# A fused Mamba and mixture-of-experts block on one core: the taps' row spread by full-height products, a lead for each spread of B, the last steps in halves, new slot tables

## What is computed

```
x  = L0_attn_x;  xn = layernorm(x)                 # 2048 tokens, 128 features
# Mamba block
xz = rmsnorm(xn) @ W_in; xi, z = split(xz)         # 256 channels each
xc = silu(conv4(xi) + conv_b)                      # causal taps along the tokens
dt, B, C = split(xc @ W_x);  dt = softplus(dt @ W_dt + b_dt)
h[t] = exp(dt * A) * h[t-1] + dt * xc * B          # 256 channels x 16 states
y  = (sum over states of h * C) + D_skip * xc
s  = xn + (y * silu(z)) @ W_out
# experts: top 2 of 8, all 8 computed, weighted by score
g  = silu(sum_e score_e * (relu(xn @ W1[e] + b1[e]) @ W2[e] + b2[e]))
out = x + s * g
```

## Time and profile before

| | us |
|---|---|
| median of 3 runs (lowest, highest) | 294.17 (293.43, 294.26) |
| the profiled execution's own time | 294.09 |
| its span, first to last instruction | 292.3 |
| busy in the span: PE, DVE, POOL, ACT | 268.1, 261.3, 241.0, 228.5 |

### The profile page before, as it was taken

The page is one execution under the profiler, slowest core; times in us unless marked ns, Lnnn a source line. Parts: engine busy times, 40 slices in busy tenths (PEclk is TensorE's granted clock), DMA queues, the critical chain, the costliest instruction groups (busy, mean ns, idle before and its releaser), DMA issues. The chain is left out here.

```text
span 292.3 us, 4275 instructions
## 1 busy us (share of the span) xinstructions
PE 268.1 (92%) x1237; PEld 137.2 (47%) x1237; DVE 261.3 (89%) x317; ACT 228.5 (78%) x444; POOL 241.0 (82%) x202
## 2 busy tenths in 40 slices
PE   7999989699999899699999999698999998999992
PEld 5543434255556345137474734124566443655461
DVE  4578999919999999979999797979999999999993
ACT  1377896989979885989998957989987875698630
POOL 5407986848999996757999999798999997799984
PEclk9999999989999999889999999899999999999998
DMA  6938672024029104724282005733049860000002
GB/s 181 278 79 192 149 177 58 2 59 102 9 54 208 31 0 108 182 71 86 51 183 64 0 2 126 162 99 61 7 100 207 189 153 0 2 0 2 2 1 72
DMA packets 18615, 25.65 MB, mean 88 GB/s; under 512 B 6440, under 2 KB 11935, under 8 KB 18592
## 3 DMA queue, kind: packets, MB, share of 16 engines
q1 hardware_dynamic: 17970, 24.71, 36.1%
q0 software_dynamic: 192, 0.52, 0.8%
q10 hardware_dynamic: 430, 0.14, 0.2%
HBM read 8.13 MB, written 1.31 MB: 32 GB/s over the span
## 5 line engine op out<-in xcount | busy, mean ns | idle before, releaser
L431 POOL TENSOR_TENSOR hc<-hs,Ct 128x1024 f32<-128x1024 f32 x63 | 149.1, 2379 | 12.6 <-DVE hs L979 12.3
L979 DVE TENSOR_TENSOR_SCAN hs<-dec,pdbu 128x1024 f32<-128x1024 f32 x64 | 144.1, 2274 | 0.9 <-POOL hc L431 0.5
L627 ACT ACTIVATE dec<-rep,negA 128x512 f32<-128x512 f32 x126 | 86.8, 723 | 3.0 <-DVE hs L979 2.3
L965 DVE TENSOR_TENSOR pdbu<-rep,px 128x1024 f32<-128x1024 f32 x62 | 73.5, 1218 | 12.4 <-PE px L1180 11.0
L1223 PEld LDWEIGHTS px<-w,hT 128*128 128x128 f32 x512 | 60.9, 192 | 17.5 <-issue 9.1
L1217 PE MATMUL px<-xnT,w 128*128 128x512 f32 x128 | 65.6, 614 | 1.6 <-DVE pdbu L965 0.9
L1223 PE MATMUL px<-w,hT 128*128 128x128 f32 x512 | 63.8, 278 | 1.3 <-ACT hT L760 0.9
L760 ACT ACTIVATE hT<-px,cols 128x512 f32<-128x512 f32 x64 | 43.9, 693 | 5.8 <-PE px L1217 5.5
L749 ACT ACTIVATE ysc<-px,score 128x128 f32<-128x128 f32 x116 | 33.1, 368 | 13.0 <-PE px L1223 12.8
L570 POOL TENSOR_TENSOR acc<-acc,ysc 128x512 f32<-128x512 f32 x29 | 37.6, 1298 | 6.5 <-ACT ysc L749 6.3
L1098 PE MATMUL py<-hc,rsel 128*32 128x512 f32 x256 | 35.6, 605 | 0.6 <-POOL hc L431 0.6
(11 more groups left out here) (171 smaller groups left out, 295.3 us busy)
## 6 DMA issues: line engine op xcount, KB each, us to landing
rep<-dt_u SPq DMA_DIRECT2D x116, 128.0 KB, 2.4
Ct<-bc_rows SPq DMA_DIRECT2D x16, 256.0 KB, 4.9
w<-in_L_ffn_W SPq DMA_DIRECT2D x1, 1024.0 KB
out<-xn SPq DMA_DIRECT2D x4, 256.0 KB, 2.5
x_sb<-in_L_attn_x SPq DMA_DIRECT2D x1, 768.0 KB, 5.6
rep<-dt_u POOLq DMA_DIRECT2D x4, 128.0 KB, 3.7
win<-in_L_attn_W_in SPq DMA_DIRECT2D x1, 256.0 KB, 3.0
bc_rows<-dtp SPq DMA_DIRECT2D x4, 64.0 KB, 1.6
```

What stands on the lines that cost most here:

```text
L431: eng.tensor_tensor(hc[:, n % HC_RING], hs[:, n % HS_RING], Ct[:, k % 2, j:j + 1, :].to_broadcast([P, 2, CH]), ALU.mult).then_inc(hc_last ...
L627: act.activation(dec[:, n % DEC_RING, i, :], rep[:, q, 0, :], ACT.Exp, scale=negA[:, q, j:j + 1])\
L965: dve.tensor_tensor(pdbu[:, at:at + 2, :], rep[:, 2 * pair:2 * pair + 2, 1, :], B[:, None, :].to_broadcast([P, 2, CH]), ALU.mult).then_inc ...
L979: dve.tensor_tensor_scan(hs[:, n % HS_RING].rearrange("p b t -> p (b t)"), dec[:, n % DEC_RING].rearrange("p b t -> p (b t)"), pdbu[:, at: ...
```

## The change

1. **Row of taps.** The buffer `hc[:, 0]`, whose first partition holds the row, is set to zero by a new first instruction of DVE; ACT's load of the row waits for it (`row_zero`), and with it the four loads behind it on ACT's queue. PE multiplies a square of ones with all 128 partitions, instead of one row with one row. The idle products are 3 instead of 6 ahead of it, and 2 new ones stand behind `tr`.
2. **DVE at the start.** The taps of channels 0 to 127 (`weigh_taps(0)`) and `rsel` go behind the first convolution.
3. **ACT at the start.** `Ln` goes ahead of the copy of B.
4. **AHEAD** becomes a list with a value for each spread, 0 to 4: nine spreads are issued one or two slots earlier (1, 12, 13, 15, 16, 18, 20, 21, 26), six one or two later (2, 8, 10, 19, 27, 31).
5. **The last chunk's end in halves of 256 tokens:** the last product with C, its reductions, the gate, `o` (one half in a bank of `pdbu`), POOL's and DVE's products and sums, and two output DMAs of half the size.
6. **Tables:** many jobs and steps move by a few slots.

```
-    "gate_y": [23, 40], "last_table": [40],
+    "gate_y": [23, 37], "last_table": [35],
...
-AHEAD = 2
+AHEAD = [2, 3, 1, 2, 2, 2, 2, 2, 1, 2, 1, 2, 3, 4, 2, 3, 3, 2, 3, 1, 4, 3, 2, 2, 2, 2, 3, 1, 2, 2, 2, 0]
...
-BUSY = {"row": 6, "xc1": 2}
+BUSY = {"row": 3, "tr": 2, "xc1": 2}
...
-    SLOTS.setdefault(4 * m - AHEAD, []).insert(0, ("B", m))
+    SLOTS.setdefault(4 * m - AHEAD[m], []).insert(0, ("B", m))
...
-            for k in range(CHUNKS):
-
-                sp.wait_ge(*((o_done, k + 1) if k < CHUNKS - 1 else (last_done, 1)))
+            for k in range(CHUNKS - 1):
+                sp.wait_ge(o_done, k + 1)
                 sp.dma_start(ov_dram[:, k * TPC:(k + 1) * TPC, :], xn[:, k]).then_inc(stored, 16)
-            sp.wait_ge(stored, 16 * CHUNKS)
+            k = CHUNKS - 1
+            for h in range(2):
+                i = slice(h * TPC // 2, (h + 1) * TPC // 2)
+                sp.wait_ge(last_done, h + 1)
+                sp.dma_start(ov_dram[:, k * TPC + i.start:k * TPC + i.stop, :], xn[:, k, i]).then_inc(stored, 16)
+            sp.wait_ge(stored, 16 * (CHUNKS + 1))
...
-            pool.tensor_tensor(s_sb[:, k, :], s_sb[:, k, :], acc[:, k % 2, :], ALU.mult).then_inc(last_sg_done, 1)
-            pool.wait_ge(last_sg_done, 1)
-            pool.tensor_tensor(s_sb[:, k, :], s_sb[:, k, :],
-                               x_sb[:, k].rearrange("p t d -> p (t d)"), ALU.add).then_inc(base_done, 1)
+            for h in range(2):
+                t = slice(h * CH // 2, (h + 1) * CH // 2)
+                pool.tensor_tensor(s_sb[:, k, t], s_sb[:, k, t], acc[:, k % 2, t], ALU.mult).then_inc(last_sg_done, 1)
+                pool.wait_ge(last_sg_done, h + 1)
+                pool.tensor_tensor(s_sb[:, k, t], s_sb[:, k, t],
+                                   x_sb[:, k].rearrange("p t d -> p (t d)")[:, t], ALU.add).then_inc(base_done, 1)
...
+            act.wait_ge(row_zero, 1)
             act.dma_start(cw_row.rearrange("p a b -> p (a b)"), conv_w.rearrange("d a k -> a (d k)")).then_inc(w_row, 16)
...
+            dve.memset(hc[:, 0, :, :], 0.0).then_inc(row_zero, 1)
...
             weigh_taps(1)
-            weigh_taps(0)
...
+            def times_C_last():
+
+                n = UNITS - 1
+                k, j, _ = place(n)
+                dve.wait_ge(scan_done, n + 1)
+                dve.wait_ge(reduced, (n - HC_RING) // 2 + 1)
+                for h in range(2):
+                    t = slice(h * CH // 2, (h + 1) * CH // 2)
+                    dve.tensor_tensor(hc[:, n % HC_RING, :, t], hs[:, n % HS_RING, :, t],
+                                      Ct[:, k % 2, j:j + 1, t].to_broadcast([P, 2, CH // 2]), ALU.mult).then_inc(hc_last, 1)
...
-                last = pe.matmul(pdbu[:, h, :], ones_row[:, :], cw_row[:, h, :], start=True, stop=True)
+                last = pe.matmul(pdbu[:, h, :], ones_sq[:, :], hc[:, 0, h, :], start=True, stop=True)
```

More of the change, by code:

```diff
@@ L79 @@
     "scale_rows": [0], "normalise": [7], "gate": [21, 21, 22, 24, 26, 26, 27, 27, 27, 27, 27, 27, 27, 27, 30],
-    "gate_e": [18], "gate_p": [21, 23, 26], "finish": [14], "gate_y": [22, 38], "far": [26, 29], "third": [19],
+    "gate_e": [18], "gate_p": [21, 23, 33], "finish": [12], "gate_y": [22, 38], "far": [26, 29], "third": [19],
 }, {
-    "gate_y": [23, 40], "last_table": [40],
+    "gate_y": [23, 37], "last_table": [35],
 }]
 START = {
-    "second": [1], "gate": [1, 2, 3, 3, 5, 5, 5, 5, 6, 6, 7, 8, 9, 9, 10], "gate_e": [0], "gate_p": [0, 8, 8],
+    "second": [1], "gate": [1, 2, 3, 4, 5, 5, 5, 5, 6, 7, 8, 8, 9, 9, 10], "gate_e": [0], "gate_p": [2, 7, 8],
     "third": [12],
 }
-AHEAD = 2
+AHEAD = [2, 3, 1, 2, 2, 2, 2, 2, 1, 2, 1, 2, 3, 4, 2, 3, 3, 2, 3, 1, 4, 3, 2, 2, 2, 2, 3, 1, 2, 2, 2, 0]
 LEAD = 2
@@ L858, in _ @@
             weigh_taps(1)
-            weigh_taps(0)
-            dve.wait_ge(consts, 4)
-            dve.tensor_reduce(rsel[:, :], ident[:, :].rearrange("p (i d) -> p d i", i=GROUP), AX.X, ALU.add)\
-                .then_inc(selected, 1)
             src = bank_of("xc0", 0)[:, :].rearrange("p (b t) -> p b t", b=BPC)
@@ L876, in _ @@
                 ins.then_inc(*((conv_step, 1) if t < TAPS - 1 else (dve_emptied, 1)))
+            weigh_taps(0)
             stats(2)
+            dve.wait_ge(consts, 4)
+            dve.tensor_reduce(rsel[:, :], ident[:, :].rearrange("p (i d) -> p d i", i=GROUP), AX.X, ALU.add)\
+                .then_inc(selected, 1)
             dve.wait_ge(expA, 1)
@@ L999, in empty @@
                     dve.wait_ge(sg_done, k)
-                    dve.tensor_tensor(acc[:, (k - 1) % 2, :], src[:, :], acc[:, k % 2, :], ALU.mult)\
-                        .then_inc(dve_emptied, 1)
+                    for h in range(2):
+                        t = slice(h * CH // 2, (h + 1) * CH // 2)
+                        if h == 0:
+                            dve.wait_ge(half_filled, 1)
+                        else:
+                            wait_filled(dve, job, k)
+                        dve.tensor_tensor(acc[:, (k - 1) % 2, t], (pdbu[:, 0], src)[h][:, t], acc[:, k % 2, t], ALU.mult)\
+                            .then_inc(half_emptied if h == 0 else dve_emptied, 1)
+                        dve.wait_ge(*((half_emptied, 1) if h == 0 else (dve_emptied, len(order_v))))
+                        dve.wait_ge(base_done, h + 1)
+                        dve.tensor_tensor(s_sb[:, k, t], s_sb[:, k, t], acc[:, (k - 1) % 2, t], ALU.add).then_inc(last_done, 1)
                     return
@@ L1094, in reduce @@
                 for n in (2 * m, 2 * m + 1):
-                    pe.wait_ge(hc_last, 1) if n == UNITS - 1 else pe.wait_ge(hc_done, n + 1)
+                    if n == UNITS - 1:
+                        for h in range(2):
+                            pe.wait_ge(hc_last, h + 1)
+                            t = slice(h * CH // 2, (h + 1) * CH // 2)
+                            for i in range(2):
+                                r = (2 * n + i) * GD % P
+                                last = pe.matmul(py[r:r + GD, 0, t], rsel[:, :], hc[:, n % HC_RING, i, t], start=False,
+                                                 stop=h == 1)
+                        continue
+                    pe.wait_ge(hc_done, n + 1)
                     for i in range(2):
@@ L1224, in fill @@
                                              start=b == 0, stop=b == HB - 1)
+                elif (job, k) == ("o", CHUNKS - 1):
+                    for b in range(DB - 1):
+                        pe.wait_ge(yg_done, DB * k + b + 1)
+                        for i in range(TPC):
+                            pe.matmul(halves[i // 2][:, i * D:(i + 1) * D], sz[:, k % 2, b, i * P:(i + 1) * P], wout[:, b, :],
+                                      start=i % 2 == 0, stop=False)
+                    for h in range(2):
+                        pe.wait_ge(*((yg_half, 1) if h == 0 else (yg_done, DB * (k + 1))))
+                        for i in (2 * h, 2 * h + 1):
+                            last = pe.matmul(halves[h][:, i * D:(i + 1) * D], sz[:, k % 2, DB - 1, i * P:(i + 1) * P],
+                                             wout[:, DB - 1, :], start=False, stop=i % 2 == 1)
+                        if h == 0:
+                            last.then_inc(half_filled, 1)
                 else:
```

44 lines of the change are left out of this document (27 added, 17 removed), and 28 rows, old and new, of the table TABLE.

## The result

| | before | changed |
|---|---|---|
| median (lowest, highest), us | 294.17 (293.43, 294.49), 9 runs | 290.66 (289.59, 293.52), 9 runs |
| the profiled execution's own time, its span | 294.09, 292.3 | 289.59, 287.8 |

The ratio of the times is 0.991 (95% interval 0.9882 to 0.9937): faster beyond the noise, by some 2.6 us. The median moved by 3.5 us, for the 5.5 of the forecast; the ratios in this document aren't those of the two medians, which would be 0.988 here. The profiled execution happens to be the quickest of the nine, so its trace shows more gain (4.5 us) than the median.

A forecast was written before the change was run, and what follows sets the result against it. DVE was taken as full from 187 us on, with PE nearest to full before that. Terms 2.2 + 0.1 + 2.6 + 1.8 + 0 - 1.2 = 5.5 off 294.1 gave 288.6 us, range 286.4 to 292.6.

The forecast's parts named there:

- Start: Up to the first scan: earlier row product and earlier full PE clock gain 2.2 us (0.7 without the clock).
- First turn: DVE's 5.99 us wait for spread 4 stays, as the order there is kept; gain 0.1 us.
- Second turn: m0b fills PE's wait for silu, PE's clock holds in dt, and DVE's waits shrink; gain 2.6 us.
- Third turn: tn and spread 19 ahead of dt, spread 20 right behind; DVE's 1.92 wait shrinks to 0.1; gain 1.8 us.
- End: The last chunk's end in halves: slower POOL, shorter DVE add and output DMA; together 0, bounds 0.5 us either way.
- New waits: Six later spreads and moved ACT and POOL steps bring small new waits; loss 1.2 us, bounds 0 and 3.
- first rival: PE's clock rises at 13.4 again and falls at the second turn; 291.8 us, chance 0.20.
- rival of the tables' own waits: New waits from the moved tables reach their upper bound of 3 us; 290.4 us, chance 0.13.
- slower one: Rival: the spreads behind a reduction wait for POOL's product with C each time; 296.4 us, chance 0.06.
- four signs: First scan after 27.4; clock 0.50 at second turn; waits over 1 us at spreads 8, 10, 19 or 27; first-turn wait lost.

The follow-up runs named there:

- e5: The changed kernel, unchanged, measured and profiled a second time: 290.80 us, ratio 0.9937 to the kernel before.
- e1: The kernel before with only parts 1 to 3 of the change (the start): 292.40 us beside 294.35, ratio 0.9948.
- e7: The kernel before with one job moved, m0b ahead of dt at the second turn: 292.91 us beside 293.59, ratio 0.9957.
- e6: The changed kernel with the last product with C in one piece again, the other halves kept: 290.04 us, ratio 0.9886 to the kernel before.
- e9: The kernel before with only the third turn's order (tn, spreads 19 and 20, v0, m0b) changed: 292.62 us beside 294.0, ratio 0.9975.
- e10: e6 with m6a moved ahead of the gate in the last chunk: 289.47 us beside 294.0 for the kernel before, ratio 0.9861.
- e11: e6 with a lead of 2 instead of 0 for spread 31: 289.50 us beside 294.0 for the kernel before, ratio 0.9885.
- e12: e6 with the moves of both e10 and e11: 289.52 us beside 294.0 for the kernel before, ratio 0.9865.
- e4: The changed kernel with the row of taps multiplied by one row of ones again instead of 128: 292.77 us, ratio 0.9959 to the kernel before.
- e2: The kernel before with only the new tables and spread leads: 292.22 us beside 294.35, ratio 0.9915.

## Why the prediction was wrong

Each point by the prediction's own terms, the gain in the first profile and in e5:

- **Start, 2.2: got 1.45 and 1.89.** The mechanism was right at each step: the row's product began at 4.15 (4.1 forecast), took 3.78 again, and brought the clock soon behind it. The size was off elsewhere. At the convolution the clock gave more than the 1.3 I had for it (the first product's stretch is 0.96 for 1.84, the eight passes 3.60 for 4.36, so 1.64), but the row's earlier start, counted with 0.8, gave 0.18 there, because the quick pace began at 10.0 and not at 9. The row's product began 0.72 earlier than before, but the first product with W_in only 0.18 (9.85 for 10.03): the two idle products that the change put ahead of it start at 9.00 at half pace, and ACT had its half of the rows ready at 9.35. That they cost 0.35 there is read from the rows; leaving them out was not tried. Of what was gained by the end of the convolution another 0.4 was lost on the way to the first scan. And the term is a chance, not a number: the same start gave first scans from 25.39 to 27.34 in eight profiles, so 0.7 to 2.7. e1 shows that the gain at the first scan reaches the end.
- **First turn, 0.1: got 0.85 and -0.31.** I took the fall of the clock there as given. It comes in one execution and not in another, at the same idle of 2.45. In both, it takes 0.3 longer from the first scan to PE's `dt` (29.79 and 29.80 for 29.48), and DVE waits 1.6 for `gs` on the way, where it waited 0.66 before (at 53.03). With the fall, that 0.3 is all that is seen.
- **Second turn, 2.6: got 1.60 and 1.57, and 0.42 to 0.48 of it is given back by unit 38.** This is the step that failed. The clock held, as I had it. But "PE is 2.6 ahead" overlooked what I had asked of every other place, what PE waits for next: `v0` needs ACT's copy of `dt`, and with `m0b` gone ahead nothing was left to cover it. The wait of 1.65 stands in the changed kernel and in e7 alike. PE's lead behind it was 0.8 (e7), not 2.6, so DVE could not use it at spread 17 and `o`; `o`'s wait even grew to 2.3 with DVE early. What is left is 1.1 to 1.2, e7 alone 1.0. The new idle can cost more: in e6 the clock fell right behind it, at 126.2, and from unit 24 to unit 38 it took 58.50, 0.9 more than in the two profiles of the changed kernel.
- **Third turn, 1.8: got 1.66 and 1.55** at unit 44; 2.0 at the spread itself (e9). The size was right. The sentence that DVE "carries the gain to the end, as long as PE keeps up" was right by its condition: PE did not quite.
- **End, 0 within 0.5: got -0.85 and -0.82**, outside my bounds. I priced POOL's halves (from 281.93 to 284.99, 3.06 with the gaps, about as forecast) and the half store, and cost the halved product with C on DVE at nothing. It was the dear one, by 1.12 (2.45 and a start like before, against 1.32), through POOL (e6). The other halves, which I did price, came within my bounds: 0.34 gained.
- **New waits, -1.2: +0.21 and -1.30** between unit 44 and the last scan. None of the six later spreads that I feared for is waited for in the first profile; 31, also on my list, is in e5, by 1.40, and in no profile in which the clock held there.

The first profile: 1.45 + 0.85 + 1.60 - 0.42 + 1.66 + 0.21 - 0.85 = 4.50. e5: 1.89 - 0.31 + 1.57 - 0.48 + 1.55 - 1.30 - 0.82 = 2.10. The median's 3.5 lies between, and 290.66 within the range of 286.4 to 292.6; it is the size of the gain that was missed. None of the four signs that I had named as proof of an error came, so they missed the one that was made: they asked for waits of DVE and for the clock, and not for PE's next wait. Against the 5.5 the first profile is off by -0.75 (start), +0.75 (first turn), -1.42 (second with what it gave back), -0.14, -0.85 (end) and +1.41 (waits), together -1.0; e5 by -0.31, -0.41, -1.51, -0.25, -0.82 and -0.10, together -3.4. Second turn and end are short in both. Behind that lies one error of method: I read the falls of the clock from one execution as part of the kernel's order, and forecast for each place that it falls or holds. At the first and the third turn they differ from execution to execution. That 290.66 lies near the first rival's 291.8 does nothing for that rival, which had the clock rise at 13.4 and fall at the second turn; neither came. Of the rival of the tables' own waits a part came, 1.40 at spread 31 when the clock had fallen. The slower one did not come.

Open stays what sets the lower group of the kernel before apart. No profile caught one of its executions; by their mean clock no fall is missing in them, rather some 3 us more of the lower level are there. Open is also whether the moves of e10, e11 and e12 are worth anything beyond e6.

## What to carry to other kernels

Where an engine is let past a wait, follow its list on to the next thing it waits for before its lead is counted; a job moved to cover one wait may have been the cover of the next. Before an instruction of DVE that runs beside one of POOL is cut in two, look at what POOL has ready: here that cost 1.1 us. And where PE idles for a microsecond or two at a time, profile a kernel more than once before taking its clock as known: a term that hangs on it is a chance, not a number.

## What was unexpected in the hardware

- A product that uses one row of the array for 3.78 us left PE at half pace; the same product with 128 rows brought full pace inside it or within 2.3 us of its end (in e4 and the changed kernel 1.06 against 0.68 and 0.59 for the first products with W_in), worth about 1.0 of the 1.40 us at the first scan (e4). In all fourteen profiles the clock was first at full between 6.7 and 10.9 with 128 rows, between 13.0 and 13.9 with one.
- The length of an idle of PE alone doesn't say whether the clock falls behind it. With 1.71 (second turn) it held in ten profiles of ten; with the shorter 1.56 to 1.58 ahead of the last chunk's reduction it fell in three of seven (e2, e4, e5); with 2.04 (third turn) in five of ten; with 2.45 (first turn) in ten of fourteen; with 2.76 and 2.85 in all eight.
- More time at the lower clock isn't more time in all: the 22 quickest executions of the kernel before have the lower mean clock (0.973 and 0.974 against 0.978 to 0.980).
- A half-width product on DVE took 1.76 us beside one of POOL, and 0.77 when it started first.
